# Layer 0's attention opening by batch, and the numerators multiplied by reciprocals on GpSimd

## The reference

```
x = x + attention0(layernorm(x), ctx)
Q = xn @ Wq + bq          # 512 -> 512, 32 heads of 16
K = ctx @ Wk + bk         # 512 -> 128, 8 key heads of 16, each for 4 query heads
V = ctx @ Wv + bv         # 512 -> 128
w = softmax(Q K^T / 4)    # per batch and head, 128 x 128
y = (w @ V) @ Wo + bo
```

## Time and profile before

| | |
|---|---|
| median of 3 runs | 1238.02 us (1235.65 to 1238.74) |
| profiled execution: its own time | 1236.24 us |
| profiled execution: span | 1234.6 us |
| PE busy in the span | 96% |
| DVE, ACT, POOL busy | 66%, 54%, 33% |
| mean granted TensorE clock | 0.993 of full |
| layer 0's attention loop | units begin at 42.5 us, its last projections are near 174 us |

### The profile page before, as it was taken

How to read it: one execution, slowest core, us unless ns; L and a number is a source line. 1 busy time by engine, 2 the same in 40 slices (tenths; PEclk the granted TensorE clock), 3 DMA queues, 4 the chain that set the end, 5 groups by cost and what they waited for, 6 DMA issues and landing times.

```text
span 1234.6 us, 16581 instructions
## 1 busy us (share of the span) xinstructions
PE 1184.4 (96%) x5948; PEld 914.7 (74%) x5948; DVE 818.9 (66%) x1543; ACT 671.0 (54%) x1562; POOL 404.5 (33%) x483
## 2 busy tenths in 40 slices
PE   8989889899999999899999999999999999999997
PEld 5645456667776777688888888877888888888765
DVE  4468977677776784756666667764566666677857
ACT  2245651577777784355555555643455555556621
POOL 3401324477777772022223232310122232322200
PEclk9899999999999999899999999999999999999999
DMA  8674322785778676212112122112211121120101
GB/s 290 173 172 134 139 91 103 284 217 102 153 203 253 150 147 181 86 59 60 60 44 69 43 61 69 61 52 54 69 59 50 44 69 60 61 69 27 59 1 68
DMA packets 72849, 127.93 MB, mean 104 GB/s; under 512 B 11640, under 2 KB 30968, under 8 KB 70072
## 3 DMA queue, kind: packets, MB, share of 16 engines
q1 hardware_dynamic: 53024, 73.90, 19.5%
q0 software_dynamic: 17296, 48.26, 15.6%
q10 hardware_dynamic: 2448, 4.72, 1.1%
HBM read 150.37 MB, written 26.48 MB: 143 GB/s over the span
## 4 chain that ended last, share of the span: by engine, by line
PE 80%; DVE 8%; DMA 5%; ACT 3%; issue 3%; SPq 1%; ACTq 0%; POOL 0%; POOLq 0%; DVEq 0%
PE bank L466 49%; PE bank L1198 11%; PE bank L1986 7%; PE bank L1962 4%; PE bank L678 2%; PE bank L1258 2%; PE bank L692 1%; DMA q0st<-m0T 1%; PE bank L2301 1%; PE bank L1219 1%; PE bank L644 1%; DMA wf_raw<-in_wffn,weight_row 1%; PE bank L659 1%; DMA x<-in_x 1%; DVE den L895 1%
## 5 line engine op out<-in xcount | busy, mean ns | idle before, releaser
L1954 POOL TENSOR_SCALAR p<-p,mx 128x256 f32<-128x256 f32 x256 | 163.2, 654 | 522.0 <-DVE mx L1948 522.0
L1165 DVE TENSOR_TENSOR wf_lo<-wf_raw,wf_hi 128x512 fp32r<-128x512 f32 x188 | 121.7, 690 | 33.4 <-ACT wf_hi L1159 28.6
L1940 ACT ACTIVATE p<-bank,mx 128x256 f32<-128x256 f32 x256 | 118.0, 485 | 10.7 <-DVE mx L1930 10.6
L466 PE MATMUL bank<-xnA_hi,w1q_hi 128*128 128x512 f32 x288 | 118.8, 413 | 3.7 <-DVE xnA_lo L460 3.2
L1159 ACT ACTIVATE wf_hi<-wf_raw 128x512 fp32r<-128x512 f32 x192 | 110.2, 626 | 9.0 <-DMA wf_raw<-in_wffn,weight_row 9.0
L466 PE MATMUL bank<-xnA_hi,w1q_lo 128*128 128x512 f32 x288 | 115.0, 399 | 0.0
L466 PE MATMUL bank<-xnA_lo,w1q_hi 128*128 128x512 f32 x288 | 114.4, 397 | 0.0
L1969 ACT ACTIVATE p1T_hi<-bank 128x512 fp32r<-128x512 f32 x128 | 75.1, 596 | 65.7 <-PE bank L1962 65.7
L1894 ACT ACTIVATE q1T_hi<-bank 128x512 fp32r<-128x512 f32 x64 | 38.2, 597 | 132.5 <-PE bank L466 132.5
L1900 DVE TENSOR_TENSOR q1T_lo<-bank,q1T_hi 128x512 fp32r<-128x512 f32 x64 | 44.2, 691 | 93.2 <-ACT q1T_hi L1894 93.2
L466 PE MATMUL bank<-w1o_hi,a1T_hi 128*128 128x512 f32 x256 | 105.2, 411 | 0.1
(11 more groups left out here) (338 smaller groups left out, 2934.3 us busy)
## 6 DMA issues: line engine op xcount, KB each, us to landing
w_raw<-in_wq SPq DMA_DIRECT2D x64, 256.0 KB
w_raw<-in_wo SPq DMA_DIRECT2D x64, 256.0 KB
moe<-xn SPq DMA_DIRECT2D x2, 2304.0 KB, 11.7
returned<-moe SPq DMA_DIRECT2D x8, 512.0 KB, 6.8
q0st<-q_rows SPq DMA_DIRECT2D x14, 256.0 KB, 4.7
x<-in_x SPq DMA_DIRECT2D x8, 256.0 KB, 5.2
ctx<-in_ctxT SPq DMA_DIRECT2D x2, 1024.0 KB, 10.6
q_rows<-q0T_hi ACTq DMA_DIRECT2D x8, 256.0 KB
```

What stands on the lines that cost most here:

```text
L466: ins = nc.tensor.matmul(ps, a, b, start=(n == 0), stop=(n == len(pairs) - 1))
L1165: nc.vector.tensor_tensor(wf[m % 2][1][:, a, c, :], raw[m % STREAMS][:, a, c, :], wf[m % 2][0][:, a, c, :].bitcast(F32), ALU.subtract).the ...
L1940: ins = nc.scalar.activation(pr1[s % 2][:, h, :], banks.of(("s1", s, n))[:, hh * 2 * P:(hh + 1) * 2 * P], ACT.Exp, bias=m[:, UH + h:UH + h ...
L1954: ins = nc.gpsimd.tensor_scalar(pr1[s % 2][:, h, :], pr1[s % 2][:, h, :], m[:, 3 * UH + h:3 * UH + h + 1], 1.0, ALU.mult, ALU.mult)
```

## The change

- The opening's work on half 0 is cut in two pieces: batch 0 (128 columns) and batches 1 to 3 (384 columns). `PIECES` lists three pieces; half 1 stays whole.
- PE's order before the loop becomes: warming, the turn of tile 0, keys and four queries of batch 0; the turns of tiles 1 to 3; keys and three queries of batches 1 to 3. DVE, ACT and the stores follow the same order; DVE takes the statistics of tiles 1 to 3 behind the low parts of batch 0's queries.
- What stood before the loop and is not in that list moves into it: `query(1, 3)` of the second piece to unit 2; the values of batches 0 to 3 and the four turns of half 1 to unit 7; half 1's keys to unit 9 and its four queries to units 11, 15, 19 and 22; the values of batches 4 to 7 to units 23 to 26, on the scores' ring of banks. Half 1's statistics on DVE stand at units 3 to 6. The split of the output weights stands at units 12 to 15.
- SP's order of loads: x's tile 0, Wk, 128 columns of the context, then Wq and the rest; batch 0's keys and queries (four loads each) ahead of half 1's x and context; `bo` and `wo` behind the maxima of batch 0.
- In the loop, DVE keeps the reciprocal; the multiply of the numerators goes to GpSimd, ahead of its own low part.

```diff
-        QUERY_AT = {KV0 + 2: 1, KV0 + 4: 2, LEAD_S + 5: 3}
+        QUERY_AT = {KV0 + 3: 0, KV0 + 7: 1, KV0 + 11: 2, KV0 + 14: 3}
+        OUT_WEIGHT_AT = {KV0 + 4 + k: k for k in range(KT)}
+        KEYS_AT, STATS1_AT = KV0 + 1, 3
+        PIECES = [(0, 0, P), (0, P, HT), (1, 0, HT)]
...
         def sync_attention0():
-            for b in range(HB):
-                load(x[:, b, :], A["x"][b]).then_inc(S[f"rows_in{b}"], 16)
-            load(wq[:, :, :], A["wq0"]).then_inc(S["ld_wq0"], 16)
+            load(x[:, 0, :], A["x"][0]).then_inc(S["rows_in0"], 16)
             load(wkv[:, 0], A["wkv0"][:, 0]).then_inc(S["ld_wk0"], 16)
-            load(ctxT[0][:, :, :], A["ctxT"][0]).then_inc(S["ld_ctx00"], 16)
+            load(ctxT[0][:, :, 0:P], A["ctxT"][0, :, :, 0:P]).then_inc(S["ld_wk0"], 16)
...
+            load(wq[:, :, :], A["wq0"]).then_inc(S["ld_wq0"], 16)
+            for b in range(1, HB):
+                load(x[:, b, :], A["x"][b]).then_inc(S[f"rows_in{b}"], 16)
+            load(ctxT[0][:, :, P:HT], A["ctxT"][0, :, :, P:HT]).then_inc(S["ld_ctx00"], 16)
...
-            for m in range(KT):
-                if m == 2:
-                    keys_in(0)
-                queries_in(0, slice(m, m + 1))
+            keys_in(0)
+            queries_in(0)
+            for b in range(HB, B):
+                load(x[:, b, :], A["x"][b]).then_inc(S["ld_x_rest"], 16)
+            load(ctxT[1][:, :, :], A["ctxT"][1]).then_inc(S["ld_ctx01"], 16)
             keys_in(1)
             queries_in(1)
             maxima(0)
+            load(bo[:, :], A["bo0"].broadcast_to([P, D])).then_inc(S["ld_wbo0"], 16)
+            load(wo_raw[:, :, :], A["wo0"]).then_inc(S["ld_wbo0"], 16)
...
-        VALUES_AT = {KV0 - 1: (HB, HB + 1), KV0: (HB + 2,), KV0 + 1: (HB + 3,)}
+        VALUES_AT = {3 * KV0 - 1 + k: HB + k for k in range(HB)}
...
         # TensorE, before the loop
+            norm_turn(0, 0, 0)
+            keys(0, 7)
+            for m, n in enumerate((4, 5, 6, 0)):
+                query(0, m, n)
+            for k in range(1, HB):
                 norm_turn(0, k, k)
-            query(0, 0, 4)
-            query(0, 1, 5)
-            keys(0, 7)
-            query(0, 2, 0)
-            query(0, 3, 1)
-            for b, n in enumerate((2, 3, 4, 5)):
-                values(b, n)
-            for k, n in enumerate((7, 2, 3, 4)):
-                norm_turn(1, k, n)
             keys(1, 5)
-            query(1, 0, 7)
+            for m, n in enumerate((7, 2, 3)):
+                query(1, m, n)
         # TensorE, in the loop
+                if j == 2:
+                    query(1, KT - 1, 4)
                 if j == KV0 - 1:
                     maxima(0)
+                    for b, n in enumerate((2, 3, 4, 5)):
+                        values(b, n)
+                    for k, n in enumerate((7, 2, 3, 4)):
+                        norm_turn(1, k, n)
+                if j == KEYS_AT:
+                    keys(2, 5)
                 if j in QUERY_AT:
-                    query(1, QUERY_AT[j], 7)
+                    query(2, QUERY_AT[j], 7)
+                if j in VALUES_AT:
+                    values(VALUES_AT[j], next(srs))
...
         # ScalarE, before the loop
+            norm_sqrt(0, 0, 1)
+            norm_hi(0, 0)
             keys(0)
             act.wait_ge(S["k0_lo"], 1)
             keys_out(nc.scalar, 0)
+            for m in range(KT):
+                query(0, m)
+                act.wait_ge(S["q0_lo"], m + 1)
+                queries_out(nc.scalar, 0, m)
+            norm_sqrt(0, 1, HB)
+            for k in range(1, HB):
+                norm_hi(0, k)
...
         # VectorE
             def divide(b, n):
                 cols = quarter(n)
                 dve.wait_ge(S["sums0"], 2 * b + 1)
-                vstep.step(nc.vector.reciprocal(den[:, cols], den[:, cols]))
-                dve.wait_ge(S["sums0"], 2 * b + 2)
-                if G0 * b + n >= 2:
-                    dve.wait_ge(S["a0_lo"], G0 * b + n - 1)
-                nc.vector.tensor_tensor(a0[:, n % 2, :], num[:, cols], den[:, cols], ALU.mult).then_inc(S["a0_norm"], 1)
+                nc.vector.reciprocal(den[:, cols], den[:, cols]).then_inc(S["a0_recip"], 1)
...
+            norm_stats(0, 0)
+            norm_recip(0, 0, 1)
+            norm_scale(0, 0)
+            keys(0)
+            for m in range(KT):
+                query(0, m)
+            for k in range(1, HB):
                 dve.wait_ge(S[f"rows_in{k}"], 16)
                 norm_stats(0, k)
-            norm_recip(0)
-            for k in range(HB):
+            norm_recip(0, 1, HB)
+            for k in range(1, HB):
                 norm_scale(0, k)
...
         # GpSimd, for each quarter n of batch b
+                    pool.wait_ge(S["a0_recip"], G0 * b + n + 1)
+                    pool.wait_ge(S["sums0"], 2 * b + 2)
+                    if G0 * b + n >= 2:
+                        pool.wait_ge(S["a0_lo"], G0 * b + n - 1)
+                    nc.gpsimd.tensor_tensor(a0[:, n % 2, :], num[:, quarter(n)], den[:, quarter(n)],
+                                            ALU.mult).then_inc(S["a0_norm"], 1)
                     if 0 < G0 * (b - 3) + n <= 4:
                         gpsimd_expert_weight(G0 * (b - 3) + n - 1)
                     pool.wait_ge(S["a0_hi"], G0 * b + n + 1)
```

More of the change, by code:

```diff
@@ L612, in tensor_attention0, with keys @@
             srs, trs, yrs = cycle((0, 1, 6)), cycle((2, 3)), cycle((7,))
-            def keys(half, n):
-                ps = banks.take(n, ("k0", half), (S["k0_lo"], half + 1))
-                pe.wait_ge(S["ld_wk0"], 16)
-                pe.wait_ge(S[f"ld_ctx0{half}"], 16)
-                mm_group(ps[:, :], [(wkv[:, 0, k, :], ctxT[half][:, k, :])
-                                    for k in range(KT)]).then_inc(S["k0_mm"], 1)
+            def keys(piece, n):
+                half, first, last = PIECES[piece]
+                ps = banks.take(n, ("k0", piece), (S["k0_lo"], piece + 1))
+                pe.wait_ge(S["ld_wk0"], 32)
+                if piece:
+                    pe.wait_ge(S[f"ld_ctx0{half}"], 16)
+                mm_group(ps[:, first:last], [(wkv[:, 0, k, :], ctxT[half][:, k, first:last])
+                                             for k in range(KT)]).then_inc(S["k0_mm"], 1)
             def values(b, n):
@@ L856, in vector_attention0, with keys @@
         def vector_attention0():
-            def keys(half):
-                dve.wait_ge(S["k_hi"], half + 1)
+            def keys(piece):
+                half, first, last = PIECES[piece]
+                dve.wait_ge(S["k_hi"], piece + 1)
                 nc.vector.scalar_tensor_tensor(
-                    out=k0T[half][1][:, :], in0=banks.of(("k0", half))[:, :], scalar=bk[:, 0:1],
-                    in1=k0T[half][0][:, :].bitcast(F32), op0=ALU.add, op1=ALU.subtract).then_inc(S["k0_lo"], 1)
+                    out=k0T[half][1][:, first:last], in0=banks.of(("k0", piece))[:, first:last], scalar=bk[:, 0:1],
+                    in1=k0T[half][0][:, first:last].bitcast(F32), op0=ALU.add,
+                    op1=ALU.subtract).then_inc(S["k0_lo"], 1)
             def values(b):
@@ L867, in values, with query @@
                                         ALU.add).then_inc(S["v0"], 1)
[L869 to L870 removed]
+            def query(piece, m):
+                half, first, last = PIECES[piece]
+                dve.wait_ge(S["q_hi"], piece * KT + m + 1)
+                of = banks.of(("q0", piece, m))[:, first:last]
                 nc.vector.scalar_tensor_tensor(
[L872 to L873 removed]
+                    out=q0T[1][:, m, first:last], in0=of, scalar=bq[:, m:m + 1],
+                    in1=q0T[0][:, m, first:last].bitcast(F32), op0=ALU.add, op1=ALU.subtract).then_inc(S["q0_lo"], 1)
             def softmax_max(i):
@@ L934, in vector_attention0 @@
                 if j == 2:
-                    query(1, 0)
-                for b in VALUES_AT.get(j, ()):
-                    values(b)
+                    query(1, KT - 1)
+                if 0 <= j - STATS1_AT < HB:
+                    if j == STATS1_AT:
+                        dve.wait_ge(S["ld_x_rest"], 16 * HB)
+                    norm_stats(1, j - STATS1_AT)
                 if j == KV0 - 1:
                     maxima(0)
+                    for b in range(HB):
+                        values(b)
+                    norm_recip(1)
+                    for k in range(HB):
+                        norm_scale(1, k)
+                if j == KEYS_AT:
+                    keys(2)
                 if j in QUERY_AT:
-                    query(1, QUERY_AT[j])
+                    query(2, QUERY_AT[j])
+                if j in VALUES_AT:
+                    values(VALUES_AT[j])
                 b = of_batch(i, LEAD_S)
```

194 lines of the change are left out of this document (88 added, 106 removed).

## The result

| | before | changed |
|---|---|---|
| median of the runs (us) | 1238.38 (1235.65 to 1240.29, 4 runs) | 1252.74 (1250.48 to 1254.65, 4 runs) |
| profiled execution: time, span | 1236.24, 1234.6 | 1252.77, 1251.3 |
| mean granted clock | 0.993 | 0.985 |

The ratio is 1.0118, with a 95% interval of 1.0102 to 1.0133: 14.4 us slower. I had said 1244.1 us and 1236 to 1251. The sign was right; the size was not, and the median lies above the range.

The account below looks back on a forecast made before the run. PE, busy 96% of the span, was taken as the bound. Terms 2.1 + 9.1 - 1.8 - 0.9 - 3.0 + 0.3 + 0.3 = +6.1 on 1238.0 gave 1244.1 us, range 1236 to 1251.

Parts of the forecast that it names:

- 9.1 of moved work: Behind unit 8: PE has 21.7 us of work beside the units instead of 12.6, which adds 9.1 us.
- 1.8 (unit 32's wait): At unit 32: PE's 1.8 us wait for its loads should vanish, counted as -1.8 us.
- 0.9 (bank 7): In the loop: a query's 0.9 us wait for its bank goes, with queries on bank 7 further apart; -0.9 us.
- its price in the last batch: In the last batch: the slower multiply on GpSimd adds 0.3 us, with bounds 0 and 1.5.
- the earlier start goes through: Rival, chance 0.14: matmuls moved into the loop run while PE would wait for DVE, keeping the first unit's 7.2 us; 1231.
- The slack takes it: Rival, chance 0.24: denser work fills 5 us more of PE's 7.6 us idle time than counted; +1, 1239 us.
- New waits: Rival, chance 0.12: late queries at unit 32 or held-back exponentials on ACT cost 2 us in each of four batches; 1252.
- To unit 8: From first unit to unit 8: 15.5 us with units 0 to 7 at DVE's pace; unit 8 at 53.0, behind by 2.1.
- an open 2 us: Before unit 8: if the earlier kernel's half clock at 45 to 51 us returns, values and turns cost 2 more.
- The gap: In the opening, before the turn of tile 1: PE idles 8.8 us, with bounds 7 and 10.
- The clock: After the opening's gap: full work at the lower clock loses 2.2 us, with the unknown 0 to 3.
- The relief of DVE: From 120 us, where DVE leads: taking the multiply off DVE returns 3.0 us, with bounds 0 and -5.

Follow-up runs that it names:

- e14: e13 with PE's keys of half 1 moved from behind unit 9 to behind unit 5; 1249.55 us, ratio 1.0099.
- e2: The kernel before with 20 idle transposes added on PE behind the scores of units 22, 25 and 28; 1240.28 us, ratio 1.0017.
- e4: The changed kernel with DVE's statistics of half 1 taken before the loop instead of at units 3 to 6; 1250.02 us, ratio 1.0101.
- e9: The changed kernel itself run again, beside the kernel before on the same chip; 1254.44 us, ratio 1.0130.
- e1: The kernel before with only the multiply of the numerators moved to GpSimd; 1236.36 us, ratio 0.9995.
- e10: The changed kernel with the multiply of the numerators put back on DVE; 1255.89 us, ratio 1.0151.
- e6: The changed kernel with the opening's gap closed: tiles 1 to 3 prepared on DVE ahead of batch 0's low parts; 1256.93 us, ratio 1.0146.
- e11: e6 with half 0's values and half 1's statistics ahead of the loop, and half 1's x loaded before batch 0's keys; 1254.43 us, ratio 1.0128.
- e15: e13 with the 1 MB load of half 1's context moved behind the loads of batch 1's queries; 1252.30 us, ratio 1.0106.
- e13: e11 with `query(1, 3)` and its stores ahead of the loop instead of behind unit 2; 1253.09 us, ratio 1.0131.
- e5: The changed kernel with the gate's and experts' first weights loaded behind batch 4's maxima instead of ahead of batch 3's; 1254.87 us, ratio 1.0131.

## Why the prediction was right in sign and wrong in size

**Right.** The mechanism: work taken out of an opening in which PE was nearly full, put behind unit 8 where PE is nearly full too. From unit 8 to batch 3's maxima the changed kernel takes 48.9 us and the kernel before 41.5, 7.4 more, and e14 shows by a run that matmuls cost their full length there. I had 9.1 of moved work less 1.8 (unit 32's wait) less 0.9 (bank 7), 6.4. Both waits are gone from PE's list over 0 to 200 us (0.2 us of the first is left), though the first came back elsewhere (see batch 3's maxima). The wait of the turns (1.05 for 1.1), 0.47 us for a multiply on GpSimd (0.46) and its price in the last batch (the last stretch is 0.14 longer, I had 0.3) came out as worked out. Of the rivals, "the earlier start goes through" had 7.2 us at the first unit, of which 4.5 came, and none was left at unit 8. "The slack takes it" is seen in e2, at half of an addition of 7 us. (Its 7.6 us of idle PE leave out 60 to 80 us, where the kernel before has 1.75 more.) "New waits" had the number, 1252, but not for its reasons: unit 32 waits only 0.21 us, and PE's waits for ACT's exponentials grow from 0.8 to 1.6 us in all, where it had 2 us in each of four batches. That its number fits is luck.

**The step that failed: "To unit 8. Units 0 to 7 go at DVE's pace, 8 x 0.69 = 5.5".** It left out what else the change puts on DVE there: four statistics of 0.86, which stand in its own diff at units 3 to 6. Unit 8 was 4.8 us late: 3.4 of statistics, of which e4 gave back 2.7; 1.65 for the values (5.35 instead of 3.70), which ran at the half clock that I named as an open 2 us and left out of the sum; 0.6 carried over from the first unit; less 0.8 by which I had overpriced the rest.

**The gap** was 10.28 instead of 8.8, outside my bound of 10 (8.26 in e9, where PE first waits 1.39 for Wq): DVE came to the statistics at 20.85, not 19.1, with one issue of a store taking 1.50 us. Pieces of 384 columns that take 2.5 us instead of 2.7, and turns of 0.44, hid this by luck, and the first unit was only 0.6 off.

**The clock was priced once.** The sum holds 2.2 us for the gap; against the kernel before, the slow clock withheld 4.1 us. It fell at four places of the stage (windows, changed kernel):

```profile
20.00:24.00 4.00, 0.00 (x0) 0.00 (x0) 2.91 (x9) 0.67 (x2) 0.00 (x0) 0.50 0.36 103
...
46.00:50.00 4.00, 0.60 (x3) 0.61 (x4) 3.19 (x7) 0.49 (x2) 0.00 (x0) 0.50 0.52 140
...
68.00:72.00 4.00, 2.65 (x6) 1.54 (x7) 1.78 (x3) 3.12 (x6) 2.61 (x3) 0.74 0.51 168
...
114.00:118.00 4.00, 3.91 (x16) 2.00 (x17) 0.68 (x2) 1.05 (x3) 0.46 (x1) 0.57 1.19 189
```

The third covers the 1.1 us by which the stretch behind unit 8 missed: a query took 5.05 us at 70.42 where it takes 3.60. It came behind waits of 0.39 and 1.30 us for DVE and ACT.

**Batch 3's maxima** are 3.1 us that no term held: PE waits 2.81 us for them where it waited 1.13, and most of the rest is the slow clock behind the wait. In both kernels the experts' weights stand right ahead of these maxima in SP's queue. The load has a wait for the values that moved to units 23 to 26, but that wait did not hold it up (DVE and SP, changed kernel):

```profile
97.82 0.28 DVE L894 TENSOR_TENSOR v<-bank,bv 128x128 f32<-128x128 f32 x1
```

```profile
102.59 0.52 SPq L564 DMA_DIRECT2D q0st<-q_rows  x1
103.22 0.44 SPq L594 DMA_DIRECT2D gate_raw<-in_gate  x1
```

The last value was added at 98.1, and SP came to these loads only at 103.2, right behind `queries_in(5)`. What changed is the distance: the maxima were issued 3.8 us behind the weights before and 3.2 now. From batch 2's maxima to batch 3's it is now 12.2 us on SP instead of 13.0, since PE no longer waits 1.8 us for unit 32. So the term "-1.8" was not a gain by itself: the next transfer in the same queue took 1.7 of it. The other traces agree (4.9 us behind the weights in e2: 0.25 of wait; 4.6 in e1: none; 2.8 in e9 and e4: 2.44 and 1.97), but no run tested the distance alone.

**The relief of DVE** was 1.5, not 3.0 (e1: 1.8; e10: 1.5). The multiply's 8 us off DVE are worth only 0.8 and 0.7 us, in the stretches behind the maxima of batches 5 and 6. I had taken 3.0 from PE's idle time behind 120 us, and the rest of that idle time had other causes. The GPSIMD Engine Reference of the Trainium skill (Specifications) would let GpSimd's two-input work and VectorE's get in each other's way through a shared interface. With the multiply gone the standing did not move to the reciprocal: its longest is 953 ns in both kernels. By the same page (Engine selection) GpSimd takes about twice as long for such work; here it is 474 ns against 290, 1.6 times.

**Why closing the gap returns so little** is what I had not seen at all. Units 0 to 7 and unit 8 have floors of their own behind the gap: batch 0's round trip through memory (34.5 us in e6), then DVE's pace, then the chain of values, turns and half 1's work, then batch 1's round trip (55.4 in e11, 51.3 in e15). Each repair that was tried uncovered the next. To end with the kernel before, the loop's 7.4 us of moved work less 1.5 of relief must be won by unit 8, which would have to start at 45 (50.9 - 7.4 + 1.5), with batch 3's collision gone too; the best variant reached 51.3.

**Open.** What decides whether a short wait costs the clock is not settled: in e11 and e15 PE waits 1.30 us at the same unit, and the query behind it takes 5.29 us in the one and 3.60 in the other. The waits in front of units 40 and 48 are put down to keys by the order of SP's issues, not by a run. The stores' round trip was shortened by moving one load; what else is in its 6.4 us was not taken apart. No run put the moved queries of half 1 back ahead of the loop, so their price rests on the marks, and on e14 for the keys. The intervals of e9, e11 and e13 overlap, so between the variants the marks decide; e4 and e14 have the lowest ratios, and even their upper ends touch the changed kernel's interval.

## What to carry to other kernels

Price a stretch that an engine sets by all that the change puts on that engine there, from the diff's own positions, before the stretch's old pace is used. Before the end of a wait for a transfer is counted as a gain, look at what stands next in the same queue: here a 32 KB transfer that PE needs stood behind one of 1.5 MB, and the time won at one wait was lost at the next. When a gap is found, work out what the next floor under it is (here a store and load through memory) before its length is counted as a gain.

## What the runs showed of the hardware that I had not expected

- A transfer of 32 KB issued 3.2 us behind one of 1.5 MB on the same queue was awaited until 6.4 us after its issue (changed kernel), and until 4.75 us after it when it was issued 3.8 us behind (kernel before); issued ahead of it (e5), PE waited for it nowhere.
- The granted clock was low also where PE was mostly busy. Windows of e15:

```profile
44.00:50.00 6.00, 3.70 (x17) 3.38 (x17) 2.98 (x8) 3.45 (x6) 0.00 (x0) 0.50 0.76 160
50.00:54.00 4.00, 1.52 (x6) 0.93 (x4) 1.29 (x2) 0.70 (x2) 0.00 (x0) 0.50 0.97 313
54.00:60.00 6.00, 5.85 (x9) 2.52 (x9) 0.00 (x0) 0.00 (x0) 0.00 (x0) 0.54 1.13 283
```

  At 54 to 60 us PE is busy for 5.85 of 6 us, at nearly the lower of its two levels (1.2 GHz).
- With eight stores of 192 KB each, it took 8.8 us from the end of the last issue to the load that waits for them with 1 MB of load beside them (e13), and 6.4 us without (e15).
